# Cross-attention and routed FFN on one core: PE's turns, the key bias product and the first block table change places

## What is computed

```
h   = layernorm(x)
Q   = h @ Wq + bq;  K = ctx @ Wk + bk;  V = ctx @ Wv + bv
s   = (Q @ K.T) / sqrt(128);  s = where(mask == 0, -1e9, s)
x1  = x + softmax(s) @ V
y   = layernorm(x1);  xn = rms_norm(y, norm_scale)
top = top_k(xn @ w_router.T, 2);  w = softmax(top values)
out = x1 + y + sum over the two experts e of w_e * down_e(u * silu(gate)),  u, gate = up_e(xn)
```

## Time and profile before

| what | us |
|---|---|
| median of three runs | 459.26 (456.94 to 460.4) |
| the profiled execution's own time | 460.92 |
| its span, first to last instruction | 459.2 |
| PE busy | 397.4 (87%) |
| DVE busy | 320.1 (70%) |
| ACT busy | 286.6 (62%) |
| POOL busy | 241.4 (53%) |

### The profile page before, as it was taken

The page is one execution under the profiler, slowest core; times in us unless marked ns, Lnnn a source line. Parts: engine busy times, 40 slices in busy tenths (PEclk is TensorE's granted clock), DMA queues, the critical chain, the costliest instruction groups (busy, mean ns, idle before and its releaser), DMA issues.

```text
span 459.2 us, 10305 instructions
## 1 busy us (share of the span) xinstructions
PE 397.4 (87%) x2742; PEld 359.9 (78%) x2742; DVE 320.1 (70%) x1294; ACT 286.6 (62%) x674; POOL 241.4 (53%) x383
## 2 busy tenths in 40 slices
PE   2479999999999999999999998187989999999960
PEld 2468899899899999999989987175878788888750
DVE  2456787887878888878878788036676676767772
ACT  1145767767667767767676656036666677777650
POOL 1063233556566566565665654116677766566670
PEclk9979999999999999999999999568899999999995
DMA  4942662573573484385276250311233653338716
GB/s 140 316 155 88 211 203 93 207 233 111 198 254 109 175 277 131 128 277 176 90 272 218 75 131 17 93 37 40 61 84 86 160 123 89 83 88 259 213 64 212
DMA packets 60823, 68.59 MB, mean 149 GB/s; under 512 B 6224, under 2 KB 52320, under 8 KB 60768
## 3 DMA queue, kind: packets, MB, share of 16 engines
q1 hardware_dynamic: 56192, 58.45, 40.7%
q0 software_dynamic: 4544, 9.38, 6.1%
q10 hardware_dynamic: 32, 0.10, 0.1%
HBM read 54.35 MB, written 13.57 MB: 148 GB/s over the span
## 4 chain that ended last, share of the span: by engine, by line
PE 67%; DVE 7%; issue 7%; DMA 7%; ACT 6%; POOL 3%; SPq 2%; POOLq 0%; ACTq 0%; DVEq 0%
PE ps L1269 18%; PE ps L1235 13%; PE ps L1383 11%; PE ps L1251 7%; PE ps L1411 6%; PE ps L1400 3%; PE ps L1356 2%; ACT attention L723 2%; DMA ctxt_in<-ctx_cols 2%; POOL parts L638 2%; DMA parts<-mbias,blk_x 2%; PE ps L1218 2%; DVE gt_high L843 2%; PE ps L1212 1%; PE ps L1220 1%
## 5 line engine op out<-in xcount | busy, mean ns | idle before, releaser
L1269 PE MATMUL ps<-attention,ctx_sb 128*128 128x128 f32 (+1 forms) x832 | 115.1, 280 | 7.6 <-ACT attention L723 3.9
L1269 PEld LDWEIGHTS ps<-attention,ctx_sb 128*128 128x128 f32 (+1 forms) x832 | 102.7, 193 | 14.0 <-issue 7.6
L638 POOL DMA_INDIRECT parts<-mbias,blk_x x78 | 78.1, 1001 | 38.8 <-ACT mbias L793 28.9
L577 POOL DMA_INDIRECT rows_in<-kept,place x64 | 81.3, 1270 | 20.3 <-issue 19.2
L723 ACT ACTIVATE attention<-ps 128x512 f32<-128x512 f32 x96 | 56.5, 597 | 38.2 <-PE ps L1251 36.4
L536 POOL TENSOR_TENSOR rstd<-ve,minus_half 128x2 f32<-128x2 f32 x32 | 23.5, 733 | 88.2 <-DVE ve L919 88.2
L1251 PE MATMUL ps<-ident,attention 128*128 128x128 f32 (+1 forms) x416 | 68.7, 281 | 0.0
L860 DVE CUSTOM_DVE_ANT_0 attention<-ps,mbias 128x1608 f32<-128x1608 f32 x32 | 58.6, 1832 | 6.3 <-issue 6.3
L700 ACT ACTIVATE attention<-attention,ebias 128x1601 f32<-128x1601 f32 x32 | 52.0, 1624 | 9.6 <-DVE ebias L878 9.6
L1174 DVE SCALAR_TENSOR_TENSOR mbias<-mbias,ps 128x256 f32<-128x256 f32 x78 | 32.8, 420 | 34.9 <-ACT mbias L780 34.2
L1235 PE MATMUL ps<-ctxt_high,gt_high 128*128 128x402 f32 x128 | 48.4, 378 | 9.2 <-DVE wr_sb L1092 6.2
(11 more groups left out here) (135 smaller groups left out, 824.0 us busy)
## 6 DMA issues: line engine op xcount, KB each, us to landing
ctxt_in<-ctx_cols SPq DMA_DIRECT2D x16, 800.5 KB, 6.3
mbias<-mbias_dram SPq DMA_DIRECT2D x16, 800.5 KB, 5.5
ctx_sb<-ctx_rows SPq DMA_DIRECT2D x16, 768.0 KB
blk_x<-rows_in SPq DMA_DIRECT2D x78, 65.0 KB, 1.9
attention<-parts SPq DMA_DIRECT2D x8, 512.0 KB, 5.0
x_in<-x SPq DMA_DIRECT2D x16, 128.0 KB, 4.5
wup_in<-w_up_t SPq DMA_DIRECT2D x8, 256.0 KB, 4.9
out<-base_all SPq DMA_DIRECT2D x8, 256.0 KB, 3.0
```

Of the source, the lines that this page charges most:

```text
L577: pool.indirect_dma_start(rows_in[g], bass.IndirectOffsetOnAxis(ap=place[:, c, u:u + 1], axis=0), kept[:, u % KEPT, c], None).then_inc(s_s ...
L638: pool.indirect_dma_start(parts, bass.IndirectOffsetOnAxis(ap=blk_x[:, m % XR, D:D + 1].bitcast(I32), axis=0), blk_y[:, m % YR], None).the ...
L1269: last = pe.matmul(ps_o[:, 0:P], ctx_sb[0:n, j, t], probs_t[0:n, t * P:(t + 1) * P], start=t == 0, stop=t == KT - 1)
```

## The change

Four edits, in the order of the code:

1. The key bias product leaves PE. At the start PE makes, in place of a column, the row Wq bk (and bq bk behind it) on all 128 partitions, and DVE copies that to `wqbk_rows` (129 columns). `xn1` gets a 129th column of ones, which POOL sets once. Per batch DVE multiplies `xn1` by `wqbk_rows` and sums along the row (`query_bias`: two fused instructions with an accumulator read each, and a small memset ahead). It stands behind the tail copy `last_probs_t` in the prep slots. L1220 on PE and L846 on DVE are gone.
2. On PE, turn group 0 goes ahead of the turn of `kept` and of the Wv product; turn group 1 goes ahead of the router product.
3. On PE, turn group 3 goes ahead of context product 1, and so ahead of `prep_gt` and of the ranking.
4. On DVE, `table_starts(0)` goes from slot 30 to slot 29.

```diff
@@ DVE
+            def query_bias(i, j):
+                b = 2 * i + j
+                dve.wait_ge(s_xn1, b + 1)
+                wait(dve, s_ebias, QT * (b - 1))
+                take_waits(5)
+                for t in range(QT):
+                    last = dve.tensor_tensor_reduce(out=xn1_wqbk[:, t], in0=xn1[:, j, t], in1=wqbk_rows[:], scale=1.0, scalar=0.0,
+                                                    op0=ALU.mult, op1=ALU.add, accum_out=qbk[:, j, t:t + 1])
+                last.then_inc(s_qbk, 1)
...
                 if is_unit(u) and prep:
                     last_probs_t(i, k)
+                if prep:
+                    query_bias(*nxt)
...
                     if u == 2 * TABLED[0] + 1:
                         table_owners(0)
-                    if u == 2 * TABLED[0] + 2:
                         table_starts(0)
@@ PE
-                pe.matmul(ps_misc[:, 0:SQ], wqk_sb[:], xt_sb[:], start=True, stop=True)
-                for t in range(QT):
-                    last = pe.matmul(ps_misc[:, SQ + t:SQ + t + 1], xt_sb[:, t * P:(t + 1) * P], side_sb[:, 1:2],
-                                     start=True, stop=True)
-                last.then_inc(s_gt, 1)
+                pe.matmul(ps_misc[:, 0:SQ], wqk_sb[:], xt_sb[:], start=True, stop=True).then_inc(s_gt, 1)
...
                 if is_unit(u + 1):
                     score(*((i, k + 1) if k < 3 else (i + 1, 0)))
+                if is_unit(u):
+                    turn(i, k, 0)
...
                 if is_unit(u):
-                    turn(i, k, 0)
+                    turn(i, k, 1)
                 if is_unit(u - 2):
                     route(i, k - 2)
-                if is_unit(u):
-                    turn(i, k, 1)
                 if prep:
                     prep_xt(*nxt, u - 1)
                 if is_unit(u):
                     times_ctx(i, k, 0)
-                if is_unit(u):
                     turn(i, k, 2)
+                    turn(i, k, 3)
                     times_ctx(i, k, 1)
```

More of the change, by code:

```diff
@@ L126, in xattn_moe @@
         wqk_sb = sb("wqk_sb", [P, D])
-        side_sb = sb("side_sb", [P, 3])
+        side_sb = sb("side_sb", [P, 1])
+        wqbk_rows = sb("wqbk_rows", [P, D + 1])
+        xn1_wqbk = sb("xn1_wqbk", [P, QT, D + 1])
         wkt_sb = sb("wkt_sb", [P, D])
@@ L149, in xattn_moe @@
         x_in = sb("x_in", [P, 2, QT, D])
-        xn1 = sb("xn1", [P, 2, QT, D])
+        xn1 = sb("xn1", [P, 2, QT, D + 1])
         ctx_sb = sb("ctx_sb", [P, 2, KT, D])
@@ L316, in xattn_moe @@
         s_gtc = sem("gt_split")
-        s_qbk = sem("qbk_copied")
+        s_qbk = sem("qbk_ready")
+        s_ones1 = sem("xn1_ones_set")
         s_pt_dve = sem("probs_t_by_dve")
@@ L583, in _ @@
             pool.memset(ident[:], 0.0).then_inc(s_pool, 1)
+            pool.memset(xn1[:, :, :, D:D + 1], 1.0).then_inc(s_ones1, 1)
             pool.memset(minus_half[:], -0.5).then_inc(s_pool, 1)
@@ L832, in ln1_norm @@
                 for t in range(QT):
-                    last = dve.tensor_scalar(xn1[:, j, t], x_in[:, j, t], mv1[:, t, 0:1], rstd1[:, t:t + 1],
+                    last = dve.tensor_scalar(xn1[:, j, t, 0:D], x_in[:, j, t], mv1[:, t, 0:1], rstd1[:, t:t + 1],
                                              ALU.subtract, ALU.mult)
@@ L843, in prep_gt @@
                 dve.tensor_scalar(gt_high[:, j], ps_misc[:, 0:SQ], side_sb[:, 0:1], None, ALU.add).then_inc(s_gth, 1)
-                wait(dve, s_ebias, QT * (b - 1))
-                dve.tensor_scalar(qbk[:, j], ps_misc[:, SQ:SQ + QT], side_sb[:, 2:3], None, ALU.add).then_inc(s_qbk, 1)
                 dve.wait_ge(s_gth, b + 1)
@@ L1080, in _ @@
             dve.tensor_copy(wqk_sb[:], ps_misc[:, 0:D])
-            dve.tensor_copy(side_sb[:], ps_misc[:, D:D + 3]).then_inc(s_wqkc, 1)
+            dve.tensor_copy(wqbk_rows[:], ps_misc[:, D:2 * D + 1])
+            dve.tensor_copy(side_sb[:], ps_misc[:, 2 * D + 1:2 * D + 2]).then_inc(s_wqkc, 1)
             ln1(0, 0)
@@ L1084, in _ @@
             prep_gt(0, 0)
+            dve.wait_ge(s_ones1, 1)
+            query_bias(0, 0)
             split_ctxt(0, 0)
@@ L1211, in prep_xt @@
                 for t in range(QT):
-                    last = pe.transpose(ps_misc[:, t * P:(t + 1) * P], xn1[:, j, t], ident[:])
+                    last = pe.transpose(ps_misc[:, t * P:(t + 1) * P], xn1[:, j, t, 0:D], ident[:])
                 last.then_inc(s_xt, 1)
@@ L1316, in slot @@
                 if is_unit(u):
-                    turn(i, k, 3)
                     times_ctx(i, k, 2)
@@ L1321, in _ @@
             pe.matmul(ps_misc[:, 0:D], wqt_sb[:], wkt_sb[:], start=True, stop=True)
[L1322 to L1325, removed]
+            pe.matmul(ps_misc[:, D:2 * D], bk_col[:].broadcast_to([P, P]), wqt_sb[:], start=True, stop=True)
+            pe.matmul(ps_misc[:, 2 * D:2 * D + 1], bq_col[:].broadcast_to([P, P]), bk_col[:], start=True, stop=True)
+            pe.matmul(ps_misc[:, 2 * D + 1:2 * D + 2], wkt_sb[:], bq_col[:], start=True, stop=True).then_inc(s_wqk, 1)
             pe.wait_ge(s_wqkc, 1)
```

## The result

The changed kernel takes 460.87 us (median; 459.27 to 463.26), the kernel before 458.54 in the same comparison: ratio 1.0048, 95% interval 1.0028 to 1.0068. That is half a per cent slower, within the one per cent that the prediction counts as the same, and 0.1 us from the 461.0 predicted. Part of that is luck: the kernel before is 0.7 us under the 459.26 from which the forecast started, so the change itself measures +2.3 us where +1.8 was forecast. The profiled execution took 462.42 us (before: 460.92). The prediction is right as a sum; its terms are not all right, as the trace shows.

What follows compares the result with a forecast made beforehand. PE bounds the attention slots (busy 77.28 of 80 us). +8.0 us until slot 29, -5.35 for the table and -0.85 in slot 31 give +1.8: 461.0 us for the median, own range 458 to 464.

Steps and rivals of the forecast that it cites:

- Odd heads: Odd slots 3 to 27 without slot 9: turns before `kept` make ACT's copy of group 0 later; 12 x 0.44 = +5.3 us.
- Prep slots: Prep slots 6 to 28: head +0.44 and tail -0.19 make +0.25 us each, 12 x 0.25 = +3.0 us.
- The head: Start of a prep slot: router product behind all eight turns, so DVE's logits reading and first context product come 0.44 us later.
- the tail: End of a prep slot: without L1220 and L846, turn 3 earlier, the last product starts at T0+4.28, 0.19 us less.
- DVE's products: Two 129-column multiplications per batch on DVE: 0.7 us taken, between 0.7 and 3.7; at 0.7 hidden in the slots.
- Start: Kernel start, nothing covers the work: L1220's 0.85 us out, multiplications, product and copy in; +0.3 us, between -0.9 and +3.3.
- Table: `table_starts` in slot 29: starts ready 5.35 us earlier by old slots, 2.65 later by clock; hole shrinks to about 4.4.
- Slot 31 and the clock: Slot 31: four turns at half clock take 0.88 us and fill PE's 0.96 us wait for ACT: -0.85 us.
- rival B: Behind the first block: the shorter hole keeps PE's clock up or restores it sooner, 3 us saved, 458.0 us; chance 0.15.
- Rival A: Slot heads: the swap of the turns is free, the heads cost nothing; -9.0 us, so 450.3 us; chance 0.20.
- rival C: Prep slot tails give nothing back, the tail copy still starting at T0+4.14; +5.0 us on the forecast, 466.0; chance 0.18.

Runs made afterwards that it cites:

- the swap alone: The kernel before with only turn groups 0 and 1 moved ahead of the `kept` turn, Wv and router products: 465.76 us, ratio 1.0138.
- once DVE waits: The changed kernel with DVE waiting for POOL's `scale` before the low half of the context in prep slots: 456.00 us, ratio 0.9916.

## Why the prediction was right, step by step

The single edits give +1.38%, +1.11%, -0.58% and -1.24%, together +0.67%, with an estimated 0.9% to either side from their four intervals; the measured +0.48% agrees, which at that width is no sharp test. In the profiled executions, slot 29 begins 8.72 us later (predicted 8.0), the first block 3.65 (2.65), and from there to the end it is 2.1 less (0.85 less). The mechanism of the swap and of the table was right. That the sum came out so near is luck: odd slots gave 1.9 us less than forecast, prep slots 2.2 more, and the expert stage made up for the rest.

- **Odd heads: mis-sized.** Twelve slots cost 3.4 us, not 5.3. The step that failed is "it comes 0.44 us later", said of the copy: it came 0.26 later (3.60 us in the slot instead of 3.34). I read the 0.72 us from L716 to L723 as ACT's own work. But the fourth turn ended at 239.56 (238.96 + 0.60), 0.10 ahead of L723, and held it; with the turns out of the way ACT needs 0.56, and 0.17 without the skip sum. `xnt` was late by 0.42, as said. Of the 0.31 us of an odd slot 0.26 is the swap's (7.94 us with the swap alone) and 0.05 comes with the early turn 3 (7.73), which was taken to cost nothing there.
- **Prep slots: the wrong price.** The head (+0.44) and the tail (-0.25, predicted -0.19; L1236 at T0+2.34 where 2.40 was said) came as worked out: +0.18 and +0.19 in slots 8 and 28, and 9.09 us in all prep slots from 6 on once DVE waits. The other ten cost 0.48 each on average, about 0.31 of it because of POOL's `scale`; the twelve together 5.2 us instead of 3.0. The step that failed is "In an odd slot turn 3 only frees DVE earlier": DVE does come free earlier there, but with that POOL's `rstd` gets longer and `scale` is caught in the next slot (464.67 us with that edit alone; see the last section). POOL, which works beside DVE, has no term in the sum.
- **DVE's products: right.** 0.28 us each, 0.21 apart, about 0.45 a batch; 0.7 was taken. Here a page and a measurement differ: by the half rate that the Trainium skill states (Vector Engine (DVE) Microarchitecture Reference, Points that are easy to get wrong) the two would have taken about 1.0, an estimate, and the rows don't bear that out for this instruction. Nor did the trace of before, against the prediction's "No row here shows it": L982, in that form with two float32 sources in SBUF, took 0.74 us for 512 columns, where twice L860's 1.14 ns a column would be 1.17 us.

```profile
252.56 0.74 DVE L982 SCALAR_TENSOR_TENSOR wup_low<-wup_in,norm_col,wup_high 128x512 fp32r<-128x512 f32 x1
```

- **Start.** The first scores came 0.06 us sooner (predicted +0.3); from there to slot 2 it took 0.63 more, 0.55 of it before slot 0. The product isn't the cause: slot 0 begins at 26.00 us before, at 25.93 with the product alone and at 26.47 with the swap alone. What differs is the pace of PE: before, the last three of the first twelve score products took 0.34 to 0.35 us each, as they do at a granted clock of 1.00 in slot 25; after, all took 0.54 or more.
- **Table: right but for the fills.** The starts were ready 3.14 us later by the clock (predicted 2.65). From there to the first block it took 10.24 us instead of 9.73, so the block came 3.65 later: issuing SP's eight fills took 5.20 us instead of 4.04, and the wait behind them, up to the load, was 0.66 shorter.
- **Slot 31 and the clock: right sign, cause open.** The turns filled the wait. But the clock is in the 2.1 us too: it came back 4.6 us behind the first block instead of 10.1, and most of slot 31 ran at 1.00, which the prediction named as the sign of rival B. B's cause, the shorter hole, isn't borne out. With the table alone the hole is 4.31 us and the clock comes back after 9.4; with the swap alone it is 10.76 us long, and the clock comes back after 6:

```profile
305.88:311.88 6.00, 5.11 (x19) 4.00 (x19) 2.27 (x10) 2.70 (x8) 0.00 (x0) 0.50 0.50 114
311.88:319.88 8.00, 6.66 (x47) 5.42 (x46) 4.51 (x27) 3.66 (x12) 3.26 (x6) 1.00 0.04 13
```

  From the first block to PE's last instruction it took 148.6 us at a mean clock of 0.94 before, 146.8 at 0.95 after, and 143.7 at 0.97 with the swap alone. A term of 1 to 2 us from this stretch can't be read from one execution of each, and how the 2.1 divides between the turns and the clock isn't shown.

Rival A (the swap is free) falls by the swap alone, rival C (the tails give nothing back) by the rows of slot 26, where the tail copy starts at T0+3.89 and not at T0+4.14.

## What to carry to other kernels

Price a moved instruction also for the engines that work beside it: here one short turn moved on PE, and the loss came from POOL, by way of DVE, a slot later. Two operations that start within 0.04 us of each other in the trace are a margin to be secured with a wait, if the wrong order is dear; 0.26 us of waiting on DVE bought up to 0.55 on PE. And before a gap between two rows of an engine is booked as its own work, look for another engine's row that ends inside the gap.

## What was not expected of the hardware

A POOL instruction on one column took 0.19 us alone and 1.77 us when it began 0.12 us behind a DVE instruction that reads two operands from SBUF; it ended with that instruction. Begun 0.04 us ahead of it, it was free. The Trainium skill has this (SBUF — State Buffer, SBUF: two separate sides): the two engines share a pair of ports as an exclusive lock, whoever starts first keeps it for the whole instruction, and a DVE instruction with two SBUF inputs takes it against a POOL operation that reads SBUF. The rows agree as to the victim on POOL. The other direction they don't show: DVE's low half lasted 1.83 to 1.84 us in the kernel before, with `scale` begun ahead of it, and 1.83 to 1.85 in the changed one where `scale` was caught.

Why `rstd` takes 0.88 instead of 0.72 us with the early turn 3 stays open, but the traces show what goes with it. It does so ten times or more in each of the seven kernels traced with that turn, and at most twice in each of the six with the turn in its old place; what starts beside it on DVE differs by 0.03 us at most. What differs is ACT. Freed from its wait for turn 3 (0.28 us in slot 25 before), DVE releases `rstd` earlier, while ACT's exponential still runs: the exponential's accumulator read starts 0.68 us behind `rstd` and not 0.33 (the rows at the head of slot 26). In the odd slots 3 to 27 of all 13 traces `rstd` took 0.86 to 0.88 us in each of the 88 cases in which that read starts 0.64 us or more behind it, and 0.70 to 0.72 in each of the 75 in which it starts at most 0.52 behind it. The other six cases are slot 7 with the early turn 3: there DVE's next two instructions start 0.06 us behind `rstd` instead of 0.03 to 0.04 ahead of it, and it took 0.72 to 0.73 us. Three of the 88 have turn 3 in its old place, two of them with ACT late by a load, so it is the moment on ACT that goes with it and not the turn as such. How ACT's work would lengthen an operation on POOL no run shows.
